# A 30-step iterated layer norm and product: TensorE turns the group six slots ahead before the slot's products instead of behind them

## The reference

```python
x = x + gnn0(layernorm(x), adj)          # 16 graphs of 512 nodes, 128 channels
x = x + ffn0(layernorm(x))
x = x + gnn1(layernorm(x), adj)          # convolution, distances, a gated update

def step(h, _):                          # the iterated part, 30 times over all 8192 rows
    h = h + 0.01 * jnp.tanh(h)
    h = h * jax.nn.sigmoid(h)
    h = _layernorm(h, ln_w, ln_b)
    h = jnp.einsum('bsc,dc->bsd', h, W) + b
    return (h, None)
x = x + scan(step, layernorm(x), length=30)
```

## Time and profile before

| | before |
|---|---|
| median of three runs | 1296.51 us (1295.51 to 1296.64) |
| time of the profiled execution | 1296.68 us |
| its span, first to last instruction | 1294.7 us |
| PE busy | 1259.3 us (97%) |
| DVE busy | 1192.7 us (92%) |
| ACT busy | 1003.3 us (77%) |
| POOL busy | 962.4 us (74%) |

### The profile page before, as it was taken

The page is one execution under the profiler, slowest core; times in us unless marked ns, Lnnn a source line. Parts: engine busy times, 40 slices in busy tenths (PEclk is TensorE's granted clock), DMA queues, the critical chain, the costliest instruction groups (busy, mean ns, idle before and its releaser), DMA issues.

```text
span 1294.7 us, 29541 instructions
## 1 busy us (share of the span) xinstructions
PE 1259.3 (97%) x9309; PEld 1123.6 (87%) x9309; DVE 1192.7 (92%) x2808; ACT 1003.3 (77%) x1408; POOL 962.4 (74%) x783
## 2 busy tenths in 40 slices
PE   8899999999999999599999999999999999999998
PEld 7677777777777777489999999999999999999998
DVE  7988888888888877899999999999999999999997
ACT  2455555555555555689999999999999999999995
POOL 2455555554555554489999999999999999999996
PEclk9999999999999999889999999999999999999999
DMA  6111111111111000000000000000000000000004
GB/s 191 42 42 41 44 51 57 51 41 40 40 40 40 0 1 1 1 2 0 0 0 0 0 0 0 0 0 0 0 0 0 0 0 0 0 0 0 0 0 130
DMA packets 29808, 27.71 MB, mean 21 GB/s; under 512 B 3285, under 2 KB 21464, under 8 KB 29656
## 3 DMA queue, kind: packets, MB, share of 16 engines
q1 hardware_dynamic: 29784, 27.41, 6.7%
HBM read 23.21 MB, written 4.19 MB: 21 GB/s over the span
## 4 chain that ended last, share of the span: by engine, by line
PE 83%; DVE 10%; issue 3%; ACT 2%; SPq 1%; POOL 0%; DVEq 0%; DMA 0%; ACTq 0%; POOLq 0%
PE psum L861 33%; PE psum L877 16%; PE psum L857 7%; PE psum L632 4%; PE psum L634 4%; PE psum L633 4%; PE psum L803 4%; PE psum L654 3%; PE psum L649 3%; DVE emb_n L1410 2%; DVE xh_mem L1233 1%; PE psum L643 1%; ACT emb_f L994 1%; PE psum L663 1%; DVE upd L1371 1%
## 5 line engine op out<-in xcount | busy, mean ns | idle before, releaser
L482 POOL TENSOR_TENSOR f_rs<-f_var,half_neg 128x8 f32<-128x8 f32 x240 | 398.0, 1658 | 32.9 <-DVE f_var L1299 14.5
L861 PEld LDWEIGHTS psum<-w_t,y_all 128*128 128x128 f32 x2880 | 382.7, 193 | 9.3
L861 PE MATMUL psum<-w_t,y_all 128*128 128x128 f32 x2880 | 388.7, 275 | 0.0
L1262 DVE BATCH_NORM_STATS2 f_stat<-g_ring 128x6 f32<-128x256 f32 x960 | 340.5, 413 | 2.5 <-ACT g_ring L931 2.4
L931 ACT ACTIVATE g_ring<-u_ring 128x1024 f32<-128x1024 f32 x240 | 328.8, 1370 | 5.5 <-DVE u_ring L1274 5.4
L954 ACT ACTIVATE y_all<-psum 128x1024 f32<-128x1024 f32 x240 | 318.6, 1327 | 9.0 <-PE psum L877 9.0
L488 POOL TENSOR_TENSOR h_ring<-g_ring,f_rs 128x640 f32<-128x640 f32 x240 | 302.7, 1261 | 18.7
L941 ACT ACTIVATE t_ring<-psum 128x1024 f32<-128x1024 f32 x232 | 309.7, 1335 | 2.9 <-PE psum L861 2.9
L1274 DVE SCALAR_TENSOR_TENSOR u_ring<-t_ring,psum 128x1024 f32<-128x1024 f32 x232 | 277.9, 1198 | 0.0
L877 PE MATMUL psum<-ident,h_ring 128*128 128x128 f32 (+1 forms) x1920 | 251.5, 274 | 9.5 <-DVE h_ring L1250 6.8
L877 PEld LDWEIGHTS psum<-ident,h_ring 128*128 128x128 f32 (+1 forms) x1920 | 231.5, 154 | 10.1 <-POOL h_ring L488 7.0
(11 more groups left out here) (193 smaller groups left out, 2136.6 us busy)
## 6 DMA issues: line engine op xcount, KB each, us to landing
work<-in_adj_dram SPq DMA_DIRECT2D x16, 1024.0 KB, 5.4
x_tok<-in_x_dram SPq DMA_DIRECT2D x16, 256.0 KB, 5.5
out_dram<-y_all SPq DMA_DIRECT2D x7, 512.0 KB, 3.2
work<-in_L_gnn_conv_w_dram SPq DMA_DIRECT2D x1, 1088.0 KB
out_dram<-y_all SPq DMA_DIRECT2D x2, 256.0 KB, 3.5
work<-in_L_gnn_w_ih_dram SPq DMA_DIRECT2D x1, 384.0 KB
work<-in_L_gnn_w_hh_dram SPq DMA_DIRECT2D x1, 192.0 KB
work<-in_L_gnn_W_dram SPq DMA_DIRECT2D x1, 64.0 KB, 5.2
```

The costliest lines, as they stand in the source:

```text
L482: pool.tensor_tensor(f_rs[:, j % 4, :], f_var[:, j % 2, :], half_neg[:, 0:GT], ALU.pow).then_inc(f_pow, 1)
L861: m = pe.matmul(y_ps[k % 2][:, h, C * t:C * t + C], y_all[:, GT * k + NT * h + t, :], w1_t[:] if t < biased else w1c_t[:], start=False, st ...
L1262: ins = dve.bn_stats(f_stat[:, j % 4, 0, 2 * q:2 * q + 2, :].rearrange("p t w -> p (t w)"), both)
```

## The change

In PE's `slot` the block that turns pair n-6 moves from behind the slot's products to ahead of them. Nothing else is edited: the lags, the waits of each block and the other engines' programs stay. The turning line is L854 in the changed kernel (L877 before), the bias products are L871 (L857), the products L875 (L861).

```diff
             def slot(it, k):
+                before = earlier(it, k, LAG_T)
+                if before is not None:
+                    i, j, s = before
+                    pe.wait_ge(f_norm, s + 1)
+                    if ACT_TILES[j]:
+                        pe.wait_ge(f_norm_act, act_norms(i, j + 1))
+                    pe.wait_ge(f_norm_dve, dve_norms(i, j) + 1)
+                    wait(pe, f_state, s - 1)
+                    for t in range(GT):
+
+                        rows = P if t < GT - DVE_TILES[j] else P - 1
+                        m = pe.transpose(g_ps[j % 2][0:rows, t // NT, P * (t % NT):P * (t % NT) + P],
+                                         tiles(h_ring[j % 4])[:, t, 0:rows], ident[:])
+                    m.then_inc(f_turn, 1)
                 if not (isinstance(it, int) and it == 0):
 
                     s = (it - 1) * GROUPS + k
...
                         if h == 0 and ends(it, ITERS) and k == GROUPS - 1:
                             m.then_inc(f_half, 1)
                     m.then_inc(f_mm, 1)
-                before = earlier(it, k, LAG_T)
-                if before is not None:
-                    i, j, s = before
-                    pe.wait_ge(f_norm, s + 1)
-                    if ACT_TILES[j]:
-                        pe.wait_ge(f_norm_act, act_norms(i, j + 1))
-                    pe.wait_ge(f_norm_dve, dve_norms(i, j) + 1)
-                    wait(pe, f_state, s - 1)
-                    for t in range(GT):
-
-                        rows = P if t < GT - DVE_TILES[j] else P - 1
-                        m = pe.transpose(g_ps[j % 2][0:rows, t // NT, P * (t % NT):P * (t % NT) + P],
-                                         tiles(h_ring[j % 4])[:, t, 0:rows], ident[:])
-                    m.then_inc(f_turn, 1)
```

## The result

The changed kernel takes 1674.7 us (median of four runs, 1674.28 to 1674.92) against 1296.52 us before: 378 us more, a ratio of 1.292 with a 95% interval of 1.291 to 1.294. The forecast was 1705 us with a range of 1670 to 1800.

What follows compares the result with a forecast made beforehand. DVE paces the 3.06 us slot; the new chain takes 3.26 + 0.12 + 0.92 + 0.39 + 0.12 = 4.81 us, 1.75 more in 231 slots; with the ends 408 us, so 1705 us, range 1670 to 1800.

Steps and rivals of the forecast that it cites:

- the chain: Within a slot: products of n, tanh of n, ACT's scale of n-5, turn of n-5, next products; 4.81 us, 77%.
- turn and products: On PE, from a turn's first weight load to the end of the following products: 3.26 us.
- end of products to tanh: From the end of PE's products to the start of a waiting tanh on ACT: 0.12 us.
- tanh to scale: On ACT, from the start of the tanh to the start of the scale: 0.92 us.
- the scale: ACT's scale itself, behind the tanh: 0.39 us, taken over 0.76 in the loaded slot and up to 1.15.
- scale's end to weight load: From the end of the last scaling to PE's first weight load of the turn: 0.12 us.
- The count and the ends: 231 slots stretch by 1.75 us each, 404 us; the start adds 3 us and the end 0.7 us.
- the sum without any release time and a few us less: How the prediction explained the lower end of its range, 1670 us.
- A: Rival: ACT's scale stays slow at 0.76 us, slot 5.18 us, 1790 us in all; with 1.15, 1880 us; 11%.
- C: Rival: ACT's scale is ready when the products end, so the turn is not held; 1296 to 1297 us; 2%.
- B: Rival: PE's clock falls to 1.2 GHz; 1855 us with a quarter of the slots, 2305 with all; 9%.
- The releaser: Sign in the profile: PE's turn waits for ACT's `h_ring` about 232 times, roughly 1.3 to 1.6 us each.

Runs made afterwards that it cites:

- e1: Changed kernel with ACT's scale of pair n-5 moved ahead of the tanh, between silu and tanh; 1349.6 us.
- e8: Changed kernel with no scaling on ACT: POOL makes six tiles and the waits for ACT's part are gone; 1339.7 us.
- e3: Changed kernel with ACT's scaled tile computed once more into an unread spare buffer, between the tanh and the real scale; 1799.2 us.
- e9: e3 with ten more transposes on PE ahead of each turn, their result overwritten by the turn; 1735.1 us.
- e10: Changed kernel with ten more transposes on PE ahead of each turn; 1668.4 us.
- e5: Kernel before with the turn of pair n-6 put between the two halves of the products of slot n; 1408.3 us.
- e2: Kernel before with ACT's scale moved between silu and tanh; 1296.5 us.
- e4: Changed kernel with POOL scaling one tile more into an unread spare buffer, ahead of its five; 1675.5 us.
- e6: Changed kernel with ACT scaling two tiles and POOL four, where it was one and five; 1801.1 us.

## Why the prediction was right

*What bounds the kernel, and the kind of the effect.* Right. The move brings the turn one pair closer, and ACT's scale behind the tanh closes the chain. Shown by e1 and e8 (take it out or away: at least 325 us return), e3 with e9 and e10 (double it: 67 us more), e5 (half the move: a third of the loss) and e2 (same edit, no effect where the distance is kept). e4 and e6 exclude POOL, the engine that the waits name.

*The slot.* Predicted 4.81 us, measured 4.685. Term by term from the timeline above:

- turn and products 905.77 to 908.38 + 0.61 = 908.99: 3.22, put at 3.26.
- end of products to tanh, 908.99 to 909.02: 0.03, put at 0.12. This is the largest error. The 0.12 came from a place where PE was at or near the half clock; both ends are modelled ends of matmuls.
- tanh to scale 0.92 and the scale 0.39, both as put. All 240 scale records average 392 ns; taking the short one of the earlier trace rows and not those of the earlier trace rows was the choice that mattered, worth up to 175 us.
- scale's end to weight load 905.70 to 905.77: 0.07, put at 0.12.

These give 4.63; the average is 4.685, since some turns start later. Where a register instruction carries the last of PE's waits (`REGISTER_ALU` with the wait on it, ahead of the turn, as in the second list of PE's queue), the release is longer: one such turn starts 0.18 us after the scale, at 901.14 against 900.57 + 0.39. PE's loop has this at three of its eight turns, and it is these three that start 0.11 us later, 0.04 us a slot in the mean. One slot in eight is 0.09 us longer besides, 0.01 in the mean, in e10 too; its cause is open. In e10 no register instruction carries these waits any more, all 129 turns between 600 and 1200 us start at 0.07, and its average is 4.64.

*The count and the ends.* 231 x (4.685 - 3.062) = 375 us; 3.3 more lie at the ends (562.3 for 559.6 at the start, 28.5 for 27.9 us behind the last tanh). Together 378.3, which is the difference of the spans, 1673.0 - 1294.7. The forecast had 404 + 4. So the mechanism and the count held. The release times were put 0.14 us too long and turn and products 0.04; the later turns, which the forecast did not have, give 0.055 back. That leaves 231 x 0.125 = 29 us of the 30 us that the forecast is off.

*The range.* It held by 5 us at its lower end, and that was partly luck. The prediction calls 1670 "the sum without any release time and a few us less", but its sum has two release times of 0.12 us, and without both it is 1705 - 231 x 0.24 = 1650 us. Only one of the two had been given bounds; both turned out too long.

*The rivals.* A, long ACT records: refuted, they vanish when ACT has idle time. C, no loss: refuted. B, the clock: it did not happen in the changed kernel (1.00 from 600 to 1200 us), but it was closer than the rows let me think. With 0.29 us more of pause in each slot (e3, e6) it cost about 60 us. My evidence against it, three windows at 61% busy and full clock, was weak: e3 is busy for 66% from 900 to 1650 us (493.40 of 750) and the clock still falls. The Trainium skill, "TensorE: Matmul & The Clock Gate", section "HAM oscillation — how this bites in real kernels", describes a clock that falls in waits of some 3 to 5 us between bursts of matmuls. In e3 and e6 the pauses were shorter, 1.90 to 2.11 us, and it fell in some slots and not in all.

*What I said the profile would show.* The tanh's spacing (4.685 for 4.8), PE's share of 68%, the short scale records and the full clock came as described. DVE's share was 69% and not 64%. The releaser did not come: I said I would be wrong in kind if the turn's wait were put down to POOL, and the profile does just that for 231 waits, of 1.49 us in the mean; its last chain has POOL in it where I expected ACT. Here the profile's naming is wrong, as e1, e3 and e4 show, and the test that I set was bad.

## What to carry to other kernels

In a hand-ordered software pipeline, count the distance between a consumer and each of its producers in every producer's own queue: "one place earlier" on one engine costs nothing only if no producer's part stands behind something that waits for this very engine's last step. When the profile names a releaser, compare its end with the waiter's start; the producer that ended 0.07 us before is the candidate, not the one that ended 0.53 us before, and loading each of the two by a known amount decides it. When a pause appears on PE, its cost is not only its length: filling it with useless transposes (e9) bought 64 us back where the clock had begun to fall, and 6 us where it had not (e10).

## What the runs showed that I had not expected

The lengths of ACT's records say little about its work when it never runs dry. The same 128x128 scale has records of 0.39 us in the changed kernel, where ACT has idle time. In the kernel before it has 0.39 at 560 us, up to 1.15 between 700 and 800 us, and 0.39 to 0.52 again between 1200 and 1250 us, though ACT is busy for all of those 50 us; the slots stay 3.06 us long. So idle time went with short records here, but short records did not need it, and why they grow and shrink is open. Start-to-start spacing (0.91 or 0.92 behind the tanh, 0.29 behind the scale) is the same in both kernels.

In the changed kernel PE's weight loads pause for 1.61 to 1.81 us ahead of each turn, in slots of 4.63 to 4.83 us, and the clock stays at 1.00 from 575 us until the last turns. In e3 and e6 the pauses are 1.90 to 2.11 us, in slots that mostly take 4.92, and the clock falls 35 and 36 times between 575 and 1770 us; such a slot took about 6.8 us (e6: tanh at 599.92 and at 606.69). Each of these falls came within 1.6 us of the end of a pause of 2.01 us or more, none so soon after one of 1.90, of which e3 has 129 at full clock. The position along the kernel is not reproducible either: the window from 36 to 40 us, the same program in both kernels, was at 1.00 in the profile before and at 0.57 to 0.58 in the one after.
